# A vision tower's last feed-forward phase: token rows written out as f16 halves, turned by transposing transfers, with the norm's scale and shift folded into the experts and four result buffers

## What is computed

```python
x = x + jax.nn.gelu(x @ mlp_w1 + mlp_b1, approximate=False) @ mlp_w2 + mlp_b2
xm = _ln(x, ln2_g, ln2_b)                    # (x - m) * rsqrt(v + EPS) * g + b
logits = xm @ gate_w.T + gate_b              # 4 experts
topv, topi = jax.lax.top_k(logits, TOPK)     # TOPK = 2
gates = jax.nn.softmax(topv, axis=-1)
...
for e in range(NEXP):
    he = jax.nn.gelu(xm @ exp_w1[e] + exp_b1[e], approximate=False)
    oe = he @ exp_w2[e] + exp_b2[e]
    moe_out = moe_out + comb[..., e:e + 1] * oe
return x + moe_out
```

## Time and profile before

| | us |
|---|---|
| median of 3 runs | 3071.34 |
| the three runs | 3059.47, 3074.27, 3071.34 |
| the profiled execution, its own time | 3069.66 |
| its span, first to last instruction | 3067.9 |

### The profile page before, as it was taken

The page is one execution under the profiler, slowest core; times in us unless marked ns, Lnnn a source line. Parts: engine busy times, 40 slices in busy tenths (PEclk is TensorE's granted clock), DMA queues, the critical chain, the costliest instruction groups (busy, mean ns, idle before and its releaser), DMA issues. The chain is left out here.

```text
span 3067.9 us, 95505 instructions
## 1 busy us (share of the span) xinstructions
PE 2735.1 (89%) x31491; PEld 2122.8 (69%) x31491; DVE 2311.6 (75%) x5324; ACT 1878.7 (61%) x3798; POOL 1686.3 (55%) x1959
## 2 busy tenths in 40 slices
PE   5888788999999999899898968999976999999998
PEld 5888555555555555555555537899965888888887
DVE  5888677787888777887787726877765777777776
ACT  5777576666666666666666636777743444444443
POOL 3667545555455666666666442566673444444444
PEclk8999899999999999999999978999988999999999
DMA  7655356576667666766767635544433444444443
GB/s 166 178 158 156 89 135 150 141 163 143 157 151 158 153 157 150 172 160 162 173 163 171 149 79 132 150 142 145 151 122 87 69 67 65 69 67 65 69 68 46
DMA packets 515433, 395.07 MB, mean 129 GB/s; under 512 B 223136, under 2 KB 488386, under 8 KB 515138
## 3 DMA queue, kind: packets, MB, share of 16 engines
q1 hardware_dynamic: 431426, 310.47, 41.3%
q0 software_dynamic: 38496, 46.38, 8.6%
q10 hardware_dynamic: 45216, 34.34, 4.7%
HBM read 232.59 MB, written 155.42 MB: 126 GB/s over the span
## 5 line engine op out<-in xcount | busy, mean ns | idle before, releaser
L892 DVE TENSOR_REDUCE a_mx<-a_mxp 98x4 f32<-98x784 f32 x768 | 747.6, 973 | 281.3 <-PE a_mxp L1092 277.9
L663 ACT ACTIVATE a_pt<-a_st 98x784 f32<-98x784 f32 x768 | 635.3, 827 | 358.9 <-PE a_st L1078 357.7
L1907 POOL DMA_INDIRECT out_dram<-f_yo,f_idg x202 | 331.8, 1643 | 413.8 <-DVE f_yo L2248 376.9
L551 POOL TENSOR_TENSOR a_cf<-a_ctxs,a_rec 128x1176 f32<-128x1176 f32 x64 | 171.6, 2681 | 453.0 <-DMA a_rec<-a_recip 453.0
L1985 ACT ACTIVATE f_hf<-f_bank,f_b1c 128x256 f32<-128x256 f32 x606 | 254.3, 473 | 236.0 <-PE f_bank L1218 235.7
L1107 PE MATMUL a_pv<-a_pt,a_vp 98*32 98x196 f32 x6144 | 360.7, 353 | 5.7 <-issue 4.2
L1078 PE MATMUL a_st<-a_qst,a_kst 49*128 49x196 f16 x3072 | 267.5, 253 | 79.6 <-DMA a_qst<-a_mrow 55.0
L2410 PE MATMUL f_bank<-f_w2h,f_hh 128*128 x1212 | 298.9, 247 | 11.2 <-DVE f_hl L2232 9.9
L2411 PE MATMUL f_bank<-f_w2h,f_hl 128*128 x1212 | 298.2, 246 | 0.0
L2412 PE MATMUL f_bank<-f_w2l,f_hh 128*128 x1212 | 298.0, 246 | 0.0
L1092 PE MATMUL a_mxp<-a_kst,a_qst 48*128 48x196 f16 x3072 | 265.0, 251 | 34.0 <-DVE a_mx L892 28.6
(11 more groups left out here) (315 smaller groups left out, 8269.0 us busy)
## 6 DMA issues: line engine op xcount, KB each, us to landing
a_rec<-a_recip SPq DMA_DIRECT2D x256, 147.0 KB, 4.9
t_rows<-in_x_dram SPq DMA_DIRECT2D x84, 392.0 KB, 6.0
a_qst<-a_qk SPq DMA_DIRECT2D x256, 110.2 KB, 3.1
a_kst<-a_qk SPq DMA_DIRECT2D x256, 110.2 KB, 3.8
f_xg<-f_listed SPq DMA_DIRECT2D x101, 264.0 KB, 2.8
a_qk<-a_qkh SPq DMA_DIRECT2D x128, 196.0 KB, 3.1
a_qk<-a_qkl SPq DMA_DIRECT2D x128, 98.0 KB, 3.3
a_qk<-a_qkh SPq DMA_DIRECT2D x128, 98.0 KB, 2.5
```

The source lines that it names most:

```text
L663: act.activation(pt[k % PT][:].rearrange("p j a t -> p j (a t)"), st_ps[0:half_t, :, 0:unit_t], ACT.Exp, scale=sm_scale).then_inc(exp_s, 1)
L892: dve.tensor_reduce(mx[:, a, :, 2 * p:2 * p + 2].rearrange("p q j -> p j q"), mx_ps[0:half_t, :, 0:unit_t].rearrange("p j (q t) -> p j q t ...
L1907: pool.indirect_dma_start(out, bass.IndirectOffsetOnAxis(ap=idg[i % 3][:, t:t + 1], axis=0), yo[i % 3][:, t, :], None, compute_op=ALU.add) ...
```

## The change

1. The rows in the lists are no longer f32. `normed` writes to a buffer of its own, `xnf` (three of them), from which PE still turns the rows for the gate. One step later ACT (`high_rows`, behind `hidden(s, 1)`) writes the high f16 half of the 192 columns into the ring, and DVE (`low_rows`, in step `s` for unit `s - 4`, behind `low_hidden(s, 1)`) writes the low half of the last 64 columns and then of the first 128. A row is now 128 high, 64 high, 64 low, 128 low f16 numbers, then gates and token number, in all 200 words in place of 264.
2. In the second pass SP issues a transposing transfer of 256 rows by 384 f16 columns straight into `xe` (three buffers of 3 x 256 columns on 128 partitions), and a small load of the last 8 words of each row into `xg`. `turn_rows`, `affine_rows` and `split_rows` are gone, and `expert_first` reads `xe`.
3. The norm's scale multiplies the experts' first weights while they are scaled and split (`g16`). Its shift goes into the experts' first bias: `fold` on PE makes 12 matmuls of one column for each of the four experts in `gate_logits` of steps 3, 6, 9 and 12, and `folded_bias` on DVE adds them.
4. `yo`, `gate` and `idg` have four buffers, and `weigh(i)` waits for the adds of tile `i - 4`.

```diff
-    DUP, COMB, ID, RW = dim, dim + tail, dim + tail + n_exp, dim + tail + n_exp + 4
+    HIGH, LOW_TAIL, LOW, META = dim, dim + tail, dim + tail + P, 400
+    WORDS = META // 2
+    COMB, ID = LOW // 2, LOW // 2 + n_exp
+    assert dim - P == tail == 64 and LOW == 3 * P and ID < WORDS
...
+        xr16 = xr.bitcast(F16)
+        xnf = [sb(f"xnf{i}", [P, 2, 256], F32) for i in range(3)]
+        g16 = sb("g16", [P, 2], F32)
...
+        xg = [sb(f"xg{i}", [P, 2, WORDS - LOW // 2], F32) for i in range(3)]
+        xe = [sb(f"xe{i}", [P, 3, T], F16) for i in range(3)]
         mine = sb("mine", [P, 2, n_exp], F32)
-        gate = [sb(f"gate{i}", [P, 2, 1], F32) for i in range(3)]
-        idg = [sb(f"idg{i}", [P, 2], U32) for i in range(3)]
-        eh = [sb(f"eh{i}", [P, 2, T], F16) for i in range(2)]
-        el = [sb(f"el{i}", [P, 2, T], F16) for i in range(2)]
-        yo = [sb(f"yo{i}", [P, 2, dim], F32) for i in range(3)]
+        gate = [sb(f"gate{i}", [P, 2, 1], F32) for i in range(4)]
+        idg = [sb(f"idg{i}", [P, 2], U32) for i in range(4)]
...
@@ -1822,9 +1829,10 @@
             sp.wait_ge(tab_s, TABLES)
             for i in range(NT):
                 at = sp.value_load(row_i[0:1, i:i + 1], min_val=0, max_val=n_exp * CAP + (SPARE - 1) * T)
-                wait(sp, tg_s, i - 2)
+                wait(sp, e1_s, 3 * (i - 2))
+                sp.dma_start_transpose(xe[i % 3][:], listed16[bass.ds(at, T), 0:LOW]).then_inc(xe_s[i % 3], 16)
                 wait(sp, gate_s, i - 2)
-                sp.dma_start(xg[i % 3][:], listed[bass.ds(at, T), :].rearrange("(t p) d -> p t d", p=P)).then_inc(xg_s[i % 3], 16)
+                sp.dma_start(xg[i % 3][:], listed[bass.ds(at, T), LOW // 2:WORDS].rearrange("(t p) d -> p t d", p=P)).then_inc(xg_s[i % 3], 16)
             sp.wait_ge(add_s[0], 16 * NT)
             sp.wait_ge(add_s[1], 16 * NT)
...
+                act.mul(g16[:], gcol[:], WSCALE).then_inc(g16_s, 1)
...
+                if n == 0:
+                    act.mul(w1h[:, f], w1f[n % 2][:], WSCALE).then_inc(w_hi, 1)
+                else:
+                    act.wait_ge(g16_s, 1)
+                    act.mul(w1h[:, f, 0], w1f[n % 2][:, 0, :], g16[:, 0:1])
+                    act.mul(w1h[:, f, 1], w1f[n % 2][:, 1, :], g16[:, 1:2]).then_inc(w_hi, 1)
...
+            def high_rows(u):
+                at = 2 * (u % RING)
+                wait(act, xn_s, XN * u + 2)
+                for j in range(4):
+                    wait(act, sc_s[j], 16 * (u - RING + 1))
+                act.copy(xr16[:, at:at + 2, 0:dim], xnf[u % 3][:, :, 0:dim]).then_inc(split_s, 1)
...
+                if 3 <= s < NU + 3:
+                    high_rows(s - 3)
...
-            def affine_rows(i):
-                wait(act, tg_s, i + 1)
-                wait(act, el_s, 2 * i)
-                for part in range(2):
-                    act.activation(xf[:, part, :], tg[i % 2][:, part * T:(part + 1) * T], ACT.Identity,
-                                   scale=gcol[:, part:part + 1], bias=bcol[:, part:part + 1]).then_inc(ef_s, 1)
...
+            act.wait_ge(bias_s, n_exp)
...
+                    for part in range(2):
+                        ins = dve.scalar_tensor_tensor(out=w1l[:, f, part], in0=w1f[n % 2][:, part, :], scalar=g16[:, part:part + 1],
+                                                       in1=w1h[:, f, part], op0=ALU.mult, op1=ALU.subtract)
+                    ins.then_inc(w_lo, 1)
...
+            def folded_bias(n):
+                f = LAYERS[n]
+                dve.wait_ge(small_in, 16 * n_small)
+                dve.wait_ge(fold_s, n)
+                dve.tensor_tensor(b1c[:, f, :], b1c[:, f, :], pg[:, 16 + CH * f:16 + CH * f + CH], ALU.add).then_inc(bias_s, 1)
...
             def normed(u):
-                at = 2 * (u % RING)
                 wait(dve, rsqrt_s, RSQRT_OPS * (u + 1))
-                for j in range(4):
-                    wait(dve, sc_s[j], 16 * (u - RING + 1))
+                wait(dve, tm_s, u - 2)
+                wait(dve, split_s, 3 * (u - 2))
                 for t in range(2):
-                    dve.tensor_scalar(xr[:, at + t, 0:dim], x4[u % 3][:, t, :], mv[:, t, 0:1], rstd[:, t:t + 1],
+                    dve.tensor_scalar(xnf[u % 3][:, t, 0:dim], x4[u % 3][:, t, :], mv[:, t, 0:1], rstd[:, t:t + 1],
                                       ALU.subtract, ALU.mult).then_inc(xn_s, 1)
                 dve.wait_ge(xn_s, XN * u + 2)
-                dve.tensor_copy(xr[:, at:at + 2, DUP:DUP + tail], xr[:, at:at + 2, P:dim]).then_inc(xn_s, 1)
+                dve.tensor_copy(xnf[u % 3][:, :, dim:256], xnf[u % 3][:, :, P:dim]).then_inc(xn_s, 1)
+
+            def low_rows(u):
+                at = 2 * (u % RING)
+                wait(dve, split_s, 3 * u + 1)
+                dve.tensor_tensor(xr16[:, at:at + 2, HIGH:LOW_TAIL], xnf[u % 3][:, :, P:dim], xr16[:, at:at + 2, P:dim],
+                                  ALU.subtract).then_inc(split_s, 1)
+                dve.tensor_tensor(xr16[:, at:at + 2, LOW_TAIL:LOW], xnf[u % 3][:, :, 0:P], xr16[:, at:at + 2, 0:P],
+                                  ALU.subtract).then_inc(split_s, 1)
 
             def logits(u):
...
+                if 4 <= s < NU + 4:
+                    low_rows(s - 4)
...
-            def split_rows(i):
-                wait(dve, ef_s, 2 * (i + 1))
-                wait(dve, e1_s, 3 * (i - 1))
-                dve.tensor_copy(eh[i % 2][:], xf[:]).then_inc(eh_s, 1)
-                dve.wait_ge(eh_s, i + 1)
-                dve.tensor_tensor(el[i % 2][:, 0, :], xf[:, 0, :], eh[i % 2][:, 0, :], ALU.subtract).then_inc(el_s, 1)
-                dve.scalar_tensor_tensor(out=el[i % 2][:, 1, :], in0=eh[i % 2][:, 1, :], scalar=lo_mask[:, 0:1], in1=xf[:, 1, :],
-                                         op0=ALU.mult, op1=ALU.add).then_inc(el_s, 1)
...
-                    wait(dve, add_s[t], 16 * (i - 2))
+                    wait(dve, add_s[t], 16 * (i - 3))
                 dve.scalar_tensor_tensor(out=mine[:], in0=expert_no[:].unsqueeze(1).to_broadcast([P, 2, n_exp]), scalar=expert_f[:, i:i + 1],
-                                         in1=xg[i % 3][:, :, COMB:ID], op0=ALU.is_equal, op1=ALU.mult).then_inc(mine_s, 1)
-                dve.tensor_copy(idg[i % 3][:], xg[i % 3][:, :, ID]).then_inc(mine_s, 1)
+                                         in1=xg[i % 3][:, :, 0:n_exp], op0=ALU.is_equal, op1=ALU.mult).then_inc(mine_s, 1)
+                dve.tensor_copy(idg[i % 4][:], xg[i % 3][:, :, n_exp]).then_inc(mine_s, 1)
                 dve.wait_ge(mine_s, 2 * (i + 1))
-                dve.tensor_reduce(gate[i % 3][:], mine[:], AX.X, ALU.add).then_inc(gate_s, 1)
...
+            def fold(n):
+                f, at = LAYERS[n], 16 + CH * LAYERS[n]
+                pe.wait_ge(w_in[n % 2], 16 * W_DMAS * (n // 2 + 1))
+                pe.wait_ge(small_in, 16 * n_small)
+                for c in range(CH):
+                    cs = slice(c * P, (c + 1) * P)
+                    pe.matmul(pg[:, at + c:at + c + 1], w1f[n % 2][:, 0, cs], bcol[:, 0:1], start=True, stop=False)
+                    ins = pe.matmul(pg[:, at + c:at + c + 1], w1f[n % 2][0:tail, 1, cs], bcol[0:tail, 1:2], start=False, stop=True)
+                ins.then_inc(fold_s, 1)
...
-            def turn_rows(i):
-                wait(pe, xg_s[i % 3], 16 * (i // 3 + 1))
-                wait(pe, ef_s, 2 * (i - 1))
-                for part in range(2):
-                    for t in range(2):
-                        ins = pe.transpose(tg[i % 2][:, part * T + t * P:part * T + (t + 1) * P], xg[i % 3][:, t, part * P:(part + 1) * P], ident[:])
-                ins.then_inc(tg_s, 1)
...
             def expert_first(i, c, e):
                 q = 3 * i + c // 2
                 if c == 0:
-                    wait(pe, el_s, 2 * (i + 1))
+                    wait(pe, xe_s[i % 3], 16 * (i // 3 + 1))
                 if c % 2 == 0:
                     wait(pe, ehf_s, 2 * q - 2)
-                cs, h, l = slice(c * P, (c + 1) * P), eh[i % 2], el[i % 2]
+                cs, x = slice(c * P, (c + 1) * P), xe[i % 3]
 
                 def weights(w, part):
                     return w[:, bass.ds(e, 1), part, cs].rearrange("p a c -> p (a c)")
 
                 ins = products(pe, p1[q % 2][:, (c % 2) * T:(c % 2) * T + T],
-                               [(weights(w1h, 0), h[:, 0, :]), (weights(w1l, 0), h[:, 0, :]), (weights(w1h, 0), l[:, 0, :]),
-                                (weights(w1h, 1), l[:, 1, :]), (weights(w1l, 1), l[:, 1, :])])
+                               [(weights(w1h, 0), x[:, 0, :]), (weights(w1l, 0), x[:, 0, :]), (weights(w1h, 0), x[:, 2, :]),
+                                (weights(w1h, 1), x[:, 1, :]), (weights(w1l, 1), x[:, 1, :])])
                 if c % 2 == 1:
```

More of the change, by code:

```diff
@@ L1616, in ffn_phase @@
         ids = sb("ids", [P, 2 * NU], F32)
[L1617 removed]
+        zrows = sb("zrows", [P, 2, WORDS], F32)
         choice = sb("choice", [P, 2, n_exp], F32)
@@ L1732, in ffn_phase @@
```

(22 more changed lines are left out.)

34 lines of the change are left out of this document (15 added, 19 removed).

## The result

The changed kernel takes 3027.99 us, the median of four runs (3016.12 to 3033.23); the kernel before, on the same chip, 3072.81 us (3059.47 to 3080.27). The ratio is 0.985, with an interval of 0.980 to 0.989. The profiled execution took 3033.23 us, its span is 3031.5.

A forecast was written before the change was run, and what follows sets the result against it. PE is near its limit in both feed-forward passes; the add loop (7.17 us) holds the second's step, PE (6.93) just behind. First add 2347 + 655 + 9.25 = 3011.6 us of span, with 1.8 around it 3013; range 2992 to 3062.

The forecast's parts named there:

- case A: Whole kernel, the forecast: both loops shorten, step 6.41 to 6.70, first pass +3 to +16, 2993 to 3034 us; chance 0.60.
- Two loops nearly equal, neither cure alone worth much: Second pass: add loop with its DVE detour (7.17 us) holds the step, PE with transposes (6.93) is 0.24 behind.
- PE's step 6.41: Second pass: with 0.52 us of transposes and the 0.2 us hole gone, PE needs 6.41 us a tile.
- The hole: Second pass: 0.2 us a step on PE before a product, waiting for a DVE product late behind `weigh`; should go.
- Add loop 6.5 at the steady landing: Second pass, four buffers: GpSimd's issues 1.88, a landing of 3.86 and 0.77 to restart give 6.5 us a step.
- jostling: Second pass: PE's 6.41 and the add loop's 6.5 are so close that the step was taken as 6.55 us.
- One sign that the forecast named: Second pass: DVE's `f_mine` would wait for no landing if the forecast was right.
- Start of the pass -4: Second pass: first add about 4 us earlier, from a shorter start (3.3 us) and first steps without turns (about 1).
- Transposing transfer: Second pass: lands in 2.85 (taken) to 6.4 us; its 192 KB take 0.73 us a step of the DMA engines.
- rival C: Second pass: the transposing transfer itself bounds, 8.4 us a tile if block by block, 3198 us in all; chance 0.10.
- `low_rows` +8: First pass: DVE's 0.67 us is hidden in plain steps, paid in 12 `choose` and free-slot steps, 8.0 us.
- Folded bias +5, of which part covered: First pass: 12 small PE products for each of 4 experts, 4 x 1.26 = 5.0 us; PE may wait there anyway.

The follow-up runs named there:

- spread folds: Changed kernel with each fold's 12 one-column products placed two behind each of the six chunks of the same step; ratio to the kernel before 0.984, again 0.980.
- late folds: Changed kernel with the folds moved to steps 46 to 49, two products behind each chunk, four raw first-weight buffers; ratio to the kernel before 0.977.
- one a step: Changed kernel with one fold chunk (two one-column products) in each of steps 14 to 37, four raw first-weight buffers; ratio to the kernel before 0.984.

## Why the prediction was right, and where it was not

The forecast was 3013 us, the time is 3028; it lies inside the range, and the kernel is faster by 1.5%, as case A had it. In part that is luck: the first pass grew by 29.6 us, nearly twice the 16 that case A allowed, and the total stayed inside A because the second pass came out 8 us better than forecast and A had room for steps of 6.70. By its steps:

- **Two loops nearly equal, neither cure alone worth much.** Shown: 7.03 with one, 7.11 with the other, 6.49 with both. The working had PE with transposes at 6.93; it is 7.03 when nothing else stops it.
- **PE's step 6.41.** Shown, 6.41 in the timeline. The hole was indeed `weigh`'s: it went from 33 waits of PE to 2.
- **Add loop 6.5 at the steady landing.** The number holds, by some luck. I had taken one tile's landing, 3.86, for the steady one, and that was the start of `f_mine`, 0.13 behind the landing at 2606.12. Before, landings from 2400 to 2900 have a mean of 3.65 us, in the changed kernel of 3.86 (median 3.7, longest 5.7). The few long ones count: 10 of the 100 steps are over 7 us, the others have a mean of 6.35, under PE's 6.41. So the two loops are again nearly equal. PE gives results every 6.41 us, with 499.31 of 500 us busy from 2400 to 2900; the adds fall behind them by 7.3 us over the pass, and that is the 0.08 between 6.41 and 6.49. The forecast of 6.55 allowed 0.05 to 0.14 for jostling; with steps of 6.49 it is 6 us better. One sign that the forecast named failed: `f_mine` does wait for landings, 11.2 us in all, since the adds run that far behind; PE stands idle 1.7 us in the whole pass.
- **Start of the pass -4.** Measured -5.5 (22.6 us from first transfer to first add, now 17.1).
- **Transposing transfer.** Lands in 3.1 us, inside the bounds of 2.85 and 6.4 and near the one taken, which rules out rival C (below). The engines' share was mis-sized: 1.3 us a tile with the small load, where I had 0.73 for the transfer alone; its own part is 1.24. I had priced by bytes a transfer that moves in 256-byte packets (768 more packets a tile). It hurt little, since the engines are half idle: with twice the transfers the step is 0.13 longer.
- **`low_rows` +8.** Measured 9.9, of which some 3 may be the clock behind two folds, so 7 to 10. It is hidden in plain steps and paid at `choose`, as worked out. The durations were right (0.28 and 0.42 us).
- **Folded bias +5, of which part covered.** This is the step that failed: 21.2 us (15 in one profile of the same code). Three errors lie in it. I read "x8" of the gate products as eight matmuls, and it is four f32 ones in two passes each; so 12 products are 24 passes, not 12. A pass took 0.155 us, not 0.105. And the clock fell behind the row, which the sum had no term for. Of the 21 us, 11 to 14 are the row with its clock (spread folds), 7 to 11 the number, partly covered in these steps. I also took 10 for 13, for cover in these steps; the folds alone measured more than either.

The changed kernel's transposing transfers (duration of SP's instruction in ns, min, median, max):

```profile
L1833 SPq DMA_TRANSPOSE f_xe<-f_listed x101: 1228/1237/2637, 2356.4 to 2989.2; - x101
...
DMA to landing us min/median/max: 2.9/3.1/4.6
```

Six blocks land in 3.1 us. By the Trainium skill's page VectorE: DVE Perf Modes (The three transpose paths) six blocks one after another would be an estimated 7.85 us; the trace disagrees, so the page's 1309 ns can't be added up block by block. By the Trainium skill's page DMA: Bandwidth & Descriptors (Latency and other measured facts), which gives 261 GB/s for a non-contiguous middle dimension, 196.6 KB would take an estimated 0.75 us; the engines' time measured here is 1.24 us, 159 GB/s.

Together: first pass 19.6 us worse than forecast, second 8 us better, and 8.1 of unedited code in that profile. That is 19.9 us of span, 3011.6 to 3031.5. The median of the four runs is 5 us under the profiled one.

What stays open: why the late folds' time is the lowest though its profile has 506 us for the first pass; and what makes the half-clock stretch behind a row longer in some profiles than in others. Between the three ways of placing the folds the timed runs don't decide. By the stages the spread folds are the best version that computes all, with a first pass 6 to 13 us under that of the four profiles whose first pass is the changed kernel's, and it beats the kernel before by 1.6 and 2.0%.

## What to carry to other kernels

Where two loops hold a step within a few tenths of each other, the removal of either shows almost nothing, and of both nearly all: work out the length of each before a cure is judged by itself, and from the mean of a landing, not its median. Small products on the bound engine are not priced by their arithmetic: count the passes of one from a row where their number is known, place them singly among large products where that engine has gaps, and look at its granted clock before calling a stretch free.

## What the runs showed of the hardware that I had not expected

- A one-column f32 product cost PE 0.28 us on the path in a pair among others and 0.31 in a row; at half clock 0.46 and 0.51. Ordinary f16 products of 192 or 256 columns take 0.08 to 0.11.
- The granted clock fell to half while PE was busy without a break, in a row of one-column products, and stayed there until 1934.56, through gate products and 3.5 us of ordinary ones. With two such products between larger ones it stayed at 1.00 or close to it through all folds of two profiles but one, ahead of which PE had been idle for 1.3 us; in the other profile the same idle time brought no fall. Of the 24 single chunks of one a step, one had a fall behind it (0.81 from 2054 to 2063), 1.23 us of idle time ahead of it.
- Behind every one of 20 rows in five profiles the clock was at half level for a while, over ten us at 0.66 to 0.70 behind 14 of them and at 0.83 behind 6; each of the latter folds was 1.5 us cheaper.
- A transposing transfer holds SP for 1.24 us (0.42 for the plain one behind it), and moves in packets of 256 bytes.
- In the tail GpSimd restarts 0.71 us after a landing that its own queue waited for; before, through DVE, it started 1.4 us after one (0.42, 0.75 and 0.27).
- Two profiles of the same code can differ by 25.5 us ahead of the part under study (1819.5 and 1845.0), which is more than half of the effect.
